# Two cross-attention layers: queries and keys as two fp32r parts in 48 rows of each partition half, scores issued in pairs

## The reference

```python
q, k_t, v_t = heads(hidden_states @ W_q), heads(text_ehs @ W_k), heads(text_ehs @ W_v)
probs_t = softmax(einsum('bhsd,bhtd->bhst', q, k_t) * attn_scale)
text_out = einsum('bhst,bhtd->bhsd', probs_t, v_t)
attn_scores = einsum('bhsd,bhnd->bhsn', q, k_ip) * attn_scale
qsem = l2norm(einsum('bhst,bte->bhse', probs_t, text_ehs))
sem = einsum('bhse,bne->bhsn', qsem, l2norm(ip_ehs))
probs_ip = softmax(attn_scores + 0.5 * sem) * spatial_mask
out = (text_out + probs_ip @ v_ip) @ W_out + b_out + residual
```

```python
out = (attend(q, k, v) + attend(q, k_ip, v_ip)) @ Wo.T + bo + residual
```

## Time and profile before

| | us |
|---|---|
| median of three runs | 3860.66 |
| time of the profiled execution | 3862.18 |
| its span, first to last instruction | 3860.4 |
| TensorE matmul (PE) busy | 3678.0 (95%), 15176 instructions |
| TensorE weight load (PEld) busy | 2187.5 (57%) |
| VectorE (DVE) busy | 1995.7 (52%) |
| ScalarE (ACT) busy | 1692.1 (44%) |
| GpSimd (POOL) busy | 816.7 (21%) |

### The profile page before, as it was taken

The page is one execution under the profiler, slowest core; times in us unless marked ns, Lnnn a source line. Parts: engine busy times, 40 slices in busy tenths (PEclk is TensorE's granted clock), DMA queues, the critical chain, the costliest instruction groups (busy, mean ns, idle before and its releaser), DMA issues.

```text
span 3860.4 us, 44608 instructions
## 1 busy us (share of the span) xinstructions
PE 3678.0 (95%) x15176; PEld 2187.5 (57%) x15176; DVE 1995.7 (52%) x4444; ACT 1692.1 (44%) x3468; POOL 816.7 (21%) x648
## 2 busy tenths in 40 slices
PE   6999999999999999999999999999999999877897
PEld 3566666665666665555665565555566655533332
DVE  4443443443433355544555565655555465656885
ACT  0232333342232345544543444444444554534786
POOL 2110000100101013122222111212211121244564
PEclk8999999999999999999999999999999999998898
DMA  4210100102251112121451111112144111139120
GB/s 157 64 60 23 45 32 25 33 26 77 49 60 66 34 46 56 30 83 40 50 85 41 42 46 45 50 27 84 45 37 34 24 34 32 30 97 71 42 57 17
DMA packets 342788, 192.77 MB, mean 50 GB/s; under 512 B 248072, under 2 KB 306264, under 8 KB 342558
## 3 DMA queue, kind: packets, MB, share of 16 engines
q1 hardware_dynamic: 342564, 189.92, 23.2%
HBM read 135.15 MB, written 53.92 MB: 49 GB/s over the span
## 4 chain that ended last, share of the span: by engine, by line
PE 79%; ACT 7%; DVE 6%; issue 3%; DMA 2%; SPq 1%; POOL 0%; POOLq 0%; ACTq 0%; DVEq 0%
PE acc L731 15%; PE acc L732 15%; PE acc L735 15%; PE score L710 5%; PE spare L783 5%; PE av L750 4%; PE av L751 4%; PE spare L831 3%; ACT prob L966 3%; PE spare L879 2%; ACT prob_hi L969 2%; PE acc L772 2%; PE spare L811 1%; DMA v_scr<-v_stage 1%; PE acc L768 1%
## 5 line engine op out<-in xcount | busy, mean ns | idle before, releaser
L966 ACT ACTIVATE prob<-score 128x512 f32<-128x512 f32 (+1 forms) x1280 | 768.1, 600 | 2046.5 <-PE score L710 2040.3
L731 PE MATMUL acc<-tok_hi,prob_hi 128*128 128x512 f32 (+1 forms) x2560 | 1286.5, 503 | 4.3 <-DVE part_f L1041 1.7
L732 PE MATMUL acc<-tok_lo,prob_hi 128*128 128x512 f32 (+1 forms) x2560 | 1015.2, 397 | 0.0
L735 PE MATMUL acc<-tok_hi,prob_lo 128*128 128x512 f32 (+1 forms) x2560 | 1007.4, 394 | 7.0 <-DVE prob_lo L1030 7.0
L969 ACT ACTIVATE prob_hi<-score 128x512 fp32r<-128x512 f32 (+1 forms) x1280 | 764.5, 597 | 0.0
L1030 DVE TENSOR_TENSOR prob_lo<-prob,prob_hi 128x512 fp32r<-128x512 f32 x880 | 648.6, 738 | 138.1 <-ACT prob_hi L969 136.8
L1259 POOL TENSOR_TENSOR prob_lo<-prob,prob_hi 128x512 fp32r<-128x512 f32 x400 | 519.6, 1311 | 842.5 <-ACT prob_hi L969 842.3
L731 PEld LDWEIGHTS acc<-tok_hi,prob_hi 128*128 128x128 f32 (+1 forms) x2560 | 498.0, 195 | 123.0 <-issue 49.2
L735 PEld LDWEIGHTS acc<-tok_hi,prob_lo 128*128 128x128 f32 (+1 forms) x2560 | 481.6, 188 | 116.2 <-DVE prob_lo L1030 7.7
L732 PEld LDWEIGHTS acc<-tok_lo,prob_hi 128*128 128x128 f32 (+1 forms) x2560 | 488.0, 191 | 93.7 <-issue 9.6
L710 PE MATMUL score<-q_ring,k_ring 102*128 102x512 bf16 (+2 forms) x1280 | 502.3, 393 | 20.1 <-ACT prob_hi L969 11.9
(11 more groups left out here) (198 smaller groups left out, 3250.5 us busy)
## 6 DMA issues: line engine op xcount, KB each, us to landing
k_ring<-k_scr SPq DMA_DIRECT2D x480, 64.0 KB
ctx_t<-in_ctxT SPq DMA_DIRECT2D x8, 2048.0 KB, 10.9
q_ring<-q_scr SPq DMA_DIRECT2D x480, 32.0 KB
v_scr<-v_stage SPq DMA_DIRECT2D x32, 410.0 KB
v_ring<-v_scr SPq DMA_DIRECT2D x40, 328.0 KB
k_scr<-part_bf SPq DMA_DIRECT2D x32, 384.0 KB, 2.5
v_scr<-v_stage SPq DMA_DIRECT2D x32, 330.0 KB
v_ring<-v_scr SPq DMA_DIRECT2D x80, 132.0 KB
```

What stands on the lines that cost most here:

```text
L731: e.matmul(acc[st][:, :], prob_hi[0:kk, ps, cols], tok_hi[0:kk, c, :], start=first, stop=False)
L732: e.matmul(acc[st][:, :], prob_hi[0:kk, ps, cols], tok_lo[0:kk, c, :], start=False, stop=False)
L735: mm = e.matmul(acc[st][:, :], prob_lo[0:kk, ps, cols], tok_hi[0:kk, c, :], start=False, stop=last)
L966: e.activation(prob[0:kk, es, :], bank_s[0:kk, :], ACT.Exp, scale=SCALE)
```

## The change

- Queries and keys are split into two fp32r parts in place of three bf16 parts: a cast and a subtraction on DVE that both read the PSUM bank, which is free after the second. POOL has no part in it.
- Three products of parts stand in 48 rows, the maxima in 2 rows (layer 0) or 4 (layer 1) below them. Rows 0 to 51 hold them for the first 512 tokens, rows 64 to 115 for the last 512. Queries are loaded into both.
- The chunks of a head come in the order of tokens 0, 4, 1, 5, 2, 6, 3, 7, so that neighbours lie in different halves. Two scores are issued one after the other, chunks n + 2 and n + 3 ahead of an even chunk n, and the pair waits until both score banks are read.
- A maxima matmul uses the 48 rows of one half. The turned maxima are split in two parts by two DVE instructions in place of five.
- Matmuls of up to 64 rows are encoded as tiles of 64 x 128 of the array, those of more rows as 128 x 128.
- The residual and the output of a unit get a place of their own in `ctx_t`, and the constant rows go from the input to DRAM scratch by DMA.

```diff
-Q_PARTS = (0, 0, 0, 1, 1, 2)
-K_PARTS = (0, 1, 2, 0, 1, 0)
+Q_PARTS = (0, 0, 1)
+K_PARTS = (0, 1, 0)
+HALF = 64
+CONST_ROW = 48
+CHUNK_AT = (0, 4, 1, 5, 2, 6, 3, 7)
-AHEAD = 3
-P_SLOTS = AHEAD + 1
+AHEAD = 2
+P_SLOTS = 4
...
-            if n + AHEAD < len(chunks):
+            if n % 2 == 0 and n + AHEAD < len(chunks):
                 o.add("score", n + AHEAD)
+                o.add("score", n + AHEAD + 1)
...
-        q_ring = sb("q_ring", [102, RING, GROUP, SQ], BF16)
-        k_ring = sb("k_ring", [102, RING, GROUP, T], BF16)
+        q_ring = sb("q_ring", [HALF + 52, RING, GROUP, SQ], F32R)
+        k_ring = sb("k_ring", [HALF + 52, RING, GROUP, T // 2], F32R)
...
-                    depth = 96 + 3 * (UNITS[u][0] + 1)
+                    row0 = HALF * (n % 2)
+                    rows = slice(row0, row0 + CONST_ROW + 2 * (UNITS[u][0] + 1))
+                    key0 = (CHUNK_AT[c] % 4) * P
...
-                    if n >= 2:
-                        e.wait_ge(s_exp, n - 1)
-                    e.matmul(score[n % 2][0:kk, :], k_ring[0:depth, slot, j, c * P:c * P + kk],
-                             q_ring[0:depth, slot, j, :], start=True, stop=True).then_inc(s_score, 1)
+                    if n >= 2 and n % 2 == 0:
+                        e.wait_ge(s_exp, n)
+                    e.matmul(score[n % 2][0:kk, :], k_ring[rows, slot, j, key0:key0 + kk],
+                             q_ring[rows, slot, j, :], start=True, stop=True).then_inc(s_score, 1)
...
-                    e.matmul(bg[:, :], q_ring[0:96, slot, j, st * P:(st + 1) * P],
-                             k_ring[0:96, slot, j, half * 512:(half + 1) * 512], start=True, stop=True).then_inc(s_bg, 1)
+                    rows = slice(HALF * half, HALF * half + CONST_ROW)
+                    e.matmul(bg[:, :], q_ring[rows, slot, j, st * P:(st + 1) * P],
+                             k_ring[rows, slot, j, :], start=True, stop=True).then_inc(s_bg, 1)
...
-                    e.tensor_copy(f, bank[bank_of[key]][0:w, 0:n]).then_inc(s_free, 1)
-                    e.wait_ge(s_free, job[key] + 1)
-                    e.tensor_copy(h[:, 0, :], f).then_inc(s_h0, 1)
...
+                    e.tensor_copy(part[0:w, i % 2, 0, :], src[0:w, :]).then_inc(s_hi, 1)
+                    e.wait_ge(s_hi, i + 1)
+                    e.tensor_tensor(part[0:w, i % 2, 1, :], src[0:w, :], part.bitcast(F32)[0:w, i % 2, 0, :],
+                                    ALU.subtract).then_inc(s_free, 1)
...
+                    for hf in range(2):
+                        at, keys = HALF * hf, slice(512 * hf, 512 * hf + 512)
+                        e.dma_start(kr[at + CONST_ROW:at + CONST_ROW + 4, slot, :, :], row_scr[:, layer, :, keys]).then_inc(s_qk[slot], 16)
+                        for i in range(3):
+                            rows = slice(at + DH * i, at + DH * i + DH)
+                            e.dma_start(kr[rows, slot, :, :],
+                                        k_scr[u, K_PARTS[i], h0 * DH:(h0 + GROUP) * DH, keys].rearrange("(h d) t -> d h t", d=DH)).then_inc(s_qk[slot], 16)
+                            e.dma_start(qr[rows, slot, :, :],
+                                        q_scr[u, Q_PARTS[i], h0 * DH:(h0 + GROUP) * DH, :].rearrange("(h d) t -> d h t", d=DH)).then_inc(s_qk[slot], 16)
```

More of the change, by code:

```diff
@@ L93, in plan @@
     now = [0]
[L94 to L99, removed]
+    urgent, bgq, current = deque(), deque(), []
+    done = dict(part=[0, 0], splits=0, vst=0, xout=[0] * NM, ctx=-1, x_in=-1, w=-1)
     def split(u, m, key):
-        settle()
         i = done["splits"]
@@ L105, in split @@
         o.add("split", u, m, key, i)
[L106 to L112, removed]
+        done["part"][i % 2] += 1
+        o.note["qk", u, m] = tuple(done["part"])
     def project(u):
@@ L235, in residual @@
         def residual(m):
-            settle()
-            o.note["residual", u, m] = (done["part"][m % 2], tuple(done["xout"]))
+            o.note["residual", u, m] = done["ctx"]
             o.add("residual", u, m)
-        tasks += [lambda: residual(0), lambda: residual(1)]
+        tasks += [lambda m=m: residual(m) for m in range(NM)]
         tasks += [(ST + 1 if layer == 0 else 1, turn(m)) for m in range(NM)]
@@ L251, in go @@
                 done["ctx"] = job
-                done["xout"][m % 2] += 1
-                if m + 2 < NM:
-                    residual(m + 2)
+                done["xout"][m] += 1
             return go
@@ L356, in plan @@
         o.add("score", n)
-        if n >= LOW_LAG:
-            o.add("low", n - LOW_LAG)
+    for n in range(AHEAD - LOW_LAG):
+        o.add("low", n)
     waiting_l1 = deque()
@@ L590, in cross_attention_pair @@
         s_vout = [sem(f"v_stored{i}") for i in range(2)]
[L591 to L592 removed]
+        s_res = [sem(f"residual_loaded{i}") for i in range(NM)]
+        s_xout = [sem(f"x_out_stored{i}") for i in range(NM)]
         s_score = sem("score_in_psum")
@@ L767, in _ @@
                         e.matmul(text[0:M, :], v_ring[0:TEXT1, slot, NT, vc], prob_hi[0:TEXT1, ps, :], start=True, stop=False)
-                    e.matmul(image[0:M, :], v_ring[:, slot, c, vc], prob_hi[:, ps, :], start=first, stop=False)
+                    e.matmul(image[0:M, :], v_ring[:, slot, CHUNK_AT[c], vc], prob_hi[:, ps, :], start=first, stop=False)
                     e.wait_ge(s_low[on_pool[n]], low_nth[n])
@@ L771, in _ @@
                         e.matmul(text[0:M, :], v_ring[0:TEXT1, slot, NT, vc], prob_lo[0:TEXT1, ps, :], start=False, stop=True)
-                    e.matmul(image[0:M, :], v_ring[:, slot, c, vc], prob_lo[:, ps, :], start=False, stop=last).then_inc(s_main, 1)
+                    e.matmul(image[0:M, :], v_ring[:, slot, CHUNK_AT[c], vc], prob_lo[:, ps, :], start=False, stop=last).then_inc(s_main, 1)
                 elif kind == "max":
@@ L1307, in _ @@
                         e.wait_ge(s_bg, max(x_job, w_job, ctx_job) + 1)
-                    if layer:
-                        e.wait_ge(s_xout[0], 16 * xouts[0])
-                        e.wait_ge(s_xout[1], 16 * xouts[1])
+                    for m in range(NM):
+                        if xouts[m]:
+                            e.wait_ge(s_xout[m], 16 * xouts[m])
                     for m in range(NM):
@@ L1428, in _ @@
             e.wait_ge(s_vout[1], 16 * (stored // 2))
-            e.wait_ge(s_xout[0], 16 * 2 * 2 * B)
-            e.wait_ge(s_xout[1], 16 * 1 * 2 * B)
+            for m in range(NM):
+                e.wait_ge(s_xout[m], 16 * 2 * B)
 def kernel(**inputs):
```

165 lines of the change are left out of this document (48 added, 117 removed).

## The result

The changed kernel takes 4397.98 us (median of four runs, 4376.7 to 4421.16); the kernel before, run beside it, 3857.97 us. The ratio is 1.14, with a 95% interval of 1.1341 to 1.146: slower by 540 us, where 513 were forecast. The profiled execution is the longest of the four, 4421.16 us with a span of 4419.1 us.

A forecast was written before the change was run, and what follows sets the result against it. TensorE's matmul count times spacing was taken as the bound up to 3354 us. Form changes 495, pairs -54, maxima spacing 12, splits 15, groups 63 to 66 0, last groups 45 sum to +513: 4374 us, range 4090 to 4500.

The forecast's parts named there:

- The bound: Up to 3354 us TensorE is busy throughout, so the time is the number of matmuls times their spacing.
- A visit at 0.39 us, 0.31 ahead of narrow weights: Cost on TensorE of a stay in the 64-row form between 128-row matmuls; 1370 more up to group 62, +495 us.
- The second score at 0.104 us: Time the second score of a pair, in another tile, adds on TensorE: 0.104 us, between 0 and 0.235.
- The pair term: 504 score pairs on TensorE before 3354 us, each 0.107 us less: -54 us, ends -106 and +12.
- Visits and pairs up to group 62: On TensorE up to 3354 us, +495 us for stays in the 64-row form and -54 us for score pairs.
- so 118 x 0.235 / 8 = 3.5 us for a pair before any visit: hidden: In mixed groups, TensorE's 3.5 us a pair hides ACT's about 2.6 us: 0 us.
- fp32r and splits: On TensorE, +12 us for maxima matmuls going to 0.235 us, +15 us (0 to 40) for stalls at query and key splits.
- The last groups: In the last 13 groups, TensorE's 288 us and ACT's 299 us, neither free of the other: +45 us (0 to +80).
- the lost double buffering: In layer 1 ACT no longer double-buffers scores; up to +20 us in the tail.
- The clock rival: Drains lower TensorE's clock too, to 0.92 throughout, some 8% more: 4680 us; chance 0.05.

The follow-up runs named there:

- e4: The changed kernel without its 64-row tiles: scores and maxima contract over both halves' rows, those between cleared; 3977.54 us, ratio 1.0303 to the kernel before.
- e8: The kernel before with the 64 rows of the last third of query projections and closing products padded to 66 with zeros; 3849.31 us, ratio 0.9965.
- e5: The kernel before, still bf16, with maxima matmuls 64 rows deep instead of 96; 4079.2 us, ratio 1.0565.
- e9: The changed kernel with both scores of a pair read from the first half's rows, so in the same 64-row tile; 4541.82 us, ratio 1.1766.
- e1: The kernel before, still bf16, with scores issued in pairs ahead of each even chunk; 3955.34 us against 3859.59, ratio 1.0242.
- e10: The kernel before in bf16 with scores in pairs in layer-0 groups alone, one by one in layer 1; 3858.99 us, ratio 0.9999.
- e7: The changed kernel with the first product of each chunk issued twice from group 66 on, 224 matmuls more; 4375.39 us, ratio 1.1326.
- e11: The changed kernel with each maxima matmul issued twice in its 64-row tile from group 68 on, 192 more; 4460.04 us, ratio 1.1514.

## Why the prediction was right, and where its terms were not

1. **The bound** (number of matmuls times their spacing up to group 62): right for the layer-0 groups. e4 changes everything but the tiles and keeps groups 2 to 17 at 1121 us. In the mixed groups it holds only while scores go one by one (point 5).
2. **A visit at 0.39 us, 0.31 ahead of narrow weights**: right, 0.385 in the changed kernel; e8 shows it from the other side, and e5 that fp32r is not its cause.
3. **The second score at 0.104 us**: mis-sized, it is 0 (e9). The pair term is -106, the low end, instead of -54.
4. **Visits and pairs up to group 62**, forecast 495 - 54 = 441 us: e4 against the changed kernel measures 348. Against e4, whose scores are fp32r as well, 495 - 504 x 0.235 = 377 were due. In groups 2 to 17 counts and prices meet: 384 visits and 128 pairs make 115 us, and 114 were measured. In groups 18 to 61 about 230 were due and 213 measured, and part of the 213 is the clock's (point 7). So a visit there costs less than its price. Some of it falls into the wait for ACT at the pair, which in e4 adds up to 49.3 us up to group 62 and in the changed kernel to 13.2:

```profile
PE score L676 <- ACT prob_hi L936: 49.3, 93, 0.9
```

   That is not all of it, for e5 has no pairs and shows the same, 0.27 against 0.18 us. What hides the rest stays open.
5. **"so 118 x 0.235 / 8 = 3.5 us for a pair before any visit: hidden", 0 us**: this step failed. e1 shows +64 in the mixed groups and +34 behind them, e10 that it is layer 1. I set TensorE's sum against ACT's sum, though the order lets neither run while the other holds the banks.
6. **fp32r and splits**, +27 up to group 62: e4 against e1 has +13.
7. **The last groups, +45, and the clock**: +133 from group 62 on. 40 are there without any visit (e4), of which the forecast gave the lost double buffering up to 20. The rest came with the tiles, and at least 38 of it with the clock by the profiled executions of e7 (23 by the medians). The clock rival had 0.05 and no part of the forecast. It was wrong in its size (4680 us) and right in its kind, and not only at the end: in groups 18 to 61 the changed kernel is at the 1.2 GHz level for 126 us, e4 for 7. The matmuls issued in those 126 us took 80 us in e4, so up to 46 us of the changed kernel's time are lost there (an estimate, since their visits are in it too).

So the visit price was right, and the total was in part luck. In the profiled executions, where the difference is 558 us, the terms were 93 us too high for the tiles and 14 for fp32r and splits, and 152 too low for the order and the last groups; some 80 of the 558 went with a clock that the forecast had left out (38 and up to 46, an estimate).

## What to carry to other kernels

Before a contraction is shortened to 64 rows so that two matmuls may share the array, count the changes of form that this makes in the stream, and price one from any short matmul that the trace already has. Here a change and back cost 0.385 us and sharing gave back 0.235, so two matmuls in a visit lose. Four would about break even by the same numbers (an estimate: two side-by-side pairs, 2 x 0.235 + 0.385 = 0.855 us, for 4 x 0.223 = 0.892). And when two buffers are released together instead of one by one, look at the engine pair that handed them back and forth: its work adds up instead of overlapping, even where both sums look small.

## What the runs showed of the hardware that was not expected

- Weight loads for two row tiles run at the same time as well as the matmuls: both loads of a pair are one row of 0.19 us, and two matmuls one row of 0.49 (0.72 in the same tile, e9).
- fp32r matmuls of 41 columns among those of 128 cost nothing. fp32 passes of 64 columns do, over all 128 rows, in the kernel before:

```profile
331.71 0.39 PE L735 MATMUL acc<-tok_hi,prob_lo 128*128 128x512 f32 x1
332.03 1.93 PE L811 MATMUL spare<-x_in,w_q 128*64 128x512 f32 x4
333.89 0.50 PE L731 MATMUL acc<-tok_hi,prob_hi 128*128 128x512 f32 x1
334.23 0.39 PE L732 MATMUL acc<-tok_lo,prob_hi 128*128 128x512 f32 x1
```

  From 331.945 (line 735 over) to 333.995 (line 731 streams) are 2.05 us for four passes that take 1.72 in the earlier trace rows: 0.33 us lost. So the price isn't one of few rows alone, and e8's padding leaves it where the weights have 64 columns. Why fp32r with 41 columns is spared stays open.
- TensorE's clock fell in the mixed groups while the rows draw it full: 58.65 of 59 us busy at 1.00, and then 34 us at the 1.2 GHz level, for 70 matmuls that took about 20 us in e4. The level changed in a wait of 1.58 us, the last row here.

```profile
2700.00:2759.00 59.00, 58.65 (x223) 34.79 (x221) 26.25 (x56) 23.89 (x52) 17.66 (x12) 1.00 0.16 48
2759.00:2793.00 34.00, 32.48 (x70) 13.04 (x70) 16.23 (x33) 18.68 (x34) 8.86 (x7) 0.51 0.18 45
2793.00:2827.00 34.00, 34.00 (x134) 21.37 (x134) 18.45 (x42) 11.69 (x26) 0.00 (x0) 0.99 0.09 23
```

```profile
2758.51 0.42 PE L733 MATMUL acc<-prob_hi,v_ring 128*33 128x512 f32 x1
2760.51 0.64 PE L737 MATMUL acc<-prob_lo,v_ring 128*33 128x512 f32 x1 [1.58 <-DVE prob_lo L993]
```

- TensorE was at its 1.2 GHz level for 291 of the last 425 us, where the same order with full rows (e4) kept 0.96. What products look like there:

```profile
4234.43 0.63 PE L733 MATMUL acc<-prob_hi,v_ring 128*33 128x512 f32 x1
4234.86 0.63 PE L736 MATMUL acc<-prob_lo,v_ring 77*33 77x512 f32 x1
4235.29 0.63 PE L737 MATMUL acc<-prob_lo,v_ring 128*33 128x512 f32 x1
```

  The products start 0.43 us apart, where they were 0.235. With 224 more full-row matmuls the clock was 0.91 (e7); 192 more half-row ones gave no time back (e11). Why the two differ stays open. The changed kernel's own four runs go with it: 4376.7 us at a mean clock of 0.955, 4421.16 us at 0.938.
